# Table writes of an expert-routing kernel go through a queue: one per turn, in steps 3 and 7 of a batch

## The chip, the cores and the metric

One core of a Trainium2 chip runs the whole program. The metric is the device time of one execution in microseconds; lower is better.

## What is computed

The input is `x` (32 batches of 112 tokens of width 256) and a context of 375 rows per batch. A gated cross-attention with 16 heads of 64 is followed by a mixture of 8 experts with the two best experts per token:

```python
x = x + tanh(g_xattn) * xattn(ctx_1024, layernorm(x))     # keys, values: context and tokens, 487 rows
xf = layernorm(x).reshape(T, D)
gate_scores = softmax(xf @ gate_w)
topk_scores, topk_idx = top_k(gate_scores, 2)
topk_scores = topk_scores / sum(topk_scores)
h = gelu(xf @ w1[e] + b1[e]);  y = h @ w2[e] + b2[e]      # for the two experts of a token
out = x + tanh(g_ffn) * (topk_scores[0] * y[topk_idx[0]] + topk_scores[1] * y[topk_idx[1]])
```

## The kernel before

The program has two stages. The **attention stage** is one loop over `STEPS`; step t holds head pair t, that is pair t % 8 of batch t // 8 (`span(t)` gives batch b and pair j, both counted from 0). All engines run the same loop, each with its own part of the work of a step, in the order in which the code is written, and they meet at semaphores. In step t:

- TensorE makes the scores of pairs t and t+1 (t even, L1125), the K and V projections of the next batch (L1107) into two alternating banks `proj_ps`, and the product with V of pair t - 4 (L1156).
- ScalarE makes the exponentials (L639), a half-precision copy of them, `p_parts` high (L648), and copies K and V out of the projection banks (L694, L708).
- VectorE takes the minimum of the negated scores for the softmax (L864) and the low halves of K and V (L933, L939), which is what frees a projection bank.
- GpSimd makes the low half of the probabilities (`p_low_of`, L510), two pairs per even step; the exponential of pair p waits for the low half of pair p - 2. It also scales and splits the attention output (L530, L516) and does parts of the normalisation: the powers L552 (step 3 of a batch) and L579 (step 7).

Some 13 to 33 steps behind a batch's first step follow its output projection, second normalisation and routing: logits, the two best experts (`top`), and then, for a **group** of batches at once, the choice (`choose`, stage `hot`), a count of how many tokens chose each expert before this one (prefix matmuls, L1210 and L1212, stage `prefix`), and the row of each token in its expert's list (`rank_entries`, L888 to L900, stage `rank`). `GROUPS` (L83) says which batches form a group, `step_of` (L86) in which step a stage of a batch stands. The prefix matmuls of a group of n batches have widths 8(n+1), 8n, ..., 8.

The stage `entry` writes the routing table to DRAM: GpSimd issues, for each batch and each of the two choices k, one indirect DMA of 112 entries (L587), 64 in all. `entries_at` (L100) puts both writes of one batch of the group into each step from the group's entry step on. The addresses `place_i` and the values `entry` are kept for every batch separately until the end, and nothing reads the table before the last write has landed.

Steps 247 to about 276 run the last batches and at the same time load and split the expert weights (VectorE L906, ScalarE L667). Then the table is read (L593), and the **tile stage** runs the experts on tiles of 256 rows: gather (L599), two layers (L1256, L1280), and accumulating indirect writes (L615).

Of the kernel before, what the change touches and what calls it, by code (L numbers as in the profile page):

```python
# [13 lines left out]
NB, LQ, LC, D = 32, 112, 375, 256  # L14
# [5 lines left out]
NP = H // 2  # L20
KT = 4
INNER = H * DH
E, TOPK, F = 8, 2, 1024
# [24 lines left out]
STEPS = range(-3 * NP, NB * NP + 20)  # L48
PAIRS = NB * NP
# [30 lines left out]
EARLY = dict(zip(STAGES, (13, 14, 15, 16, 17, 18, 19, 20, 21, 22, 23, 23, 24, 25)))  # L80
LATE = dict(USUAL, hot=27, share=28, prefix=28, rank=29, entry=30)

GROUPS = ((0, 8), (8, 16), (16, 24), (24, 28), (28, 30), (30, 31), (31, 32))  # L83


def step_of(stage, b):  # L86

    return NP * b + (EARLY if b >= NB - 2 else LATE if b == NB - 3 else USUAL)[stage]
# [6 lines left out]
def groups_at(stage, t):  # L95

    return [n for n, (first, last) in enumerate(GROUPS) if step_of(stage, last - 1) == t]


def entries_at(t):  # L100

    return [first + t - step_of("entry", last - 1) for first, last in GROUPS if 0 <= t - step_of("entry", last - 1) < last - first]


PART_STEPS = sorted([NP * b + 5 for b in range(28)] + [NP * b + 1 for b in (4, 8, 12, 16)])
CHAIN = NP * 28

# [13 lines left out]
def program(nc, x, ctx_in, g_x, g_f, ln_m_g, ln_m_b, ln_l_g, ln_l_b, wq, wkv, wout, gate_w, w1, b1, w2, b2, out):  # L121
# [3 lines left out]
    table = dram("table_dram", [TABLE_ROWS, ROWS])  # L125
    with ExitStack() as st:  # L126
# [118 lines left out]
        place_i = sb("place_i", [128, NB, TOPK], I32)  # L245
        entry = sb("entry", [128, NB, TOPK, 2])
# [128 lines left out]
        def _(sp):  # L375
            def load(b):
                s = b % 2
                sp.dma_start(ctx_sb[0:CP, s], ctx_in[b].rearrange("(t p) d -> p t d", p=CP)).then_inc(ctx_loaded[s], 16)
                sp.dma_start(x_sb[0:LQ, s], x[b]).then_inc(ctx_loaded[s], 16)
# [33 lines left out]
            for t in STEPS:  # L413
# [17 lines left out]
                if j == 7 and b + 5 >= 2 and is_batch(b + 5):  # L431

                    sp.wait_ge(pool_step, subtracted(b + 3))
                    load(b + 5)
                if t + 2 in PART_STEPS:
                    n = PART_STEPS.index(t + 2)
                    if n >= 1:
# [38 lines left out]
        def _(pool):  # L476
# [42 lines left out]
            for t in STEPS:  # L519
# [14 lines left out]
                if j in (4, 6) and is_batch(nb):  # L534
                    k = (j - 4) // 2
# [9 lines left out]
                if j == 3 and is_batch(nb):  # L545
                    first = POOL_BASE + POOL_COUNT * nb
# [26 lines left out]
                for ob in batches_at("rstd2", t):  # L573
# [3 lines left out]
                    pool.tensor_tensor(rstd2[0:LQ, s, 0:1], moments2[0:LQ, s, 1:2], eps[0:LQ, 0:1], ALU.add).then_inc(rstd2_done, 1)  # L577
                    pool.wait_ge(rstd2_done, 2 * ob + 1)
                    pool.tensor_tensor(rstd2[0:LQ, s, 1:2], rstd2[0:LQ, s, 0:1], half[0:LQ, 0:1], ALU.pow).then_inc(rstd2_done, 1)  # L579
                for ob in entries_at(t):  # L580

                    n = [first <= ob < last for first, last in GROUPS].index(True)
                    if ob == 0:
                        pool.wait_ge(filled, 32)
                    pool.wait_ge(rank_done, n + 1)
                    for k in range(TOPK):
                        pool.indirect_dma_start(table.rearrange("r (n w) -> (r n) w", w=2), bass.IndirectOffsetOnAxis(ap=place_i[0:LQ, ob, k:k + 1], axis=0),  # L587
                                                entry[0:LQ, ob, k], None).then_inc(entered, 16)

            pool.wait_ge(row_known, 1)  # L590
            pool.wait_ge(entered, NB * TOPK * 16)
# [34 lines left out]
        def _(act):  # L626
# [42 lines left out]
            for t in STEPS:  # L669
# [51 lines left out]
                for n in groups_at("share", t):  # L721
                    first, last = GROUPS[n]
                    act.wait_ge(hot_done, n + 1)
# [36 lines left out]
        def _(dve):  # L760
# [106 lines left out]
            def choose(group):  # L867

                first, last = GROUPS[group]
                n = last - first  # L870
                if group >= 1:
# [3 lines left out]
                                         ALU.is_equal))  # L875
                if group >= 1 and n < GROUPS[group - 1][1] - GROUPS[group - 1][0]:
                    dve.memset(member[0:LQ, n], 0.0)
# [30 lines left out]
            for t in STEPS:  # L908
# [77 lines left out]
                if j == 1 and is_batch(nb):  # L986
# [7 lines left out]
                    last.then_inc(moments_done, 1)  # L994
                if t in PART_STEPS:
                    part = PART_STEPS.index(t)
                    dve.wait_ge(part_loaded, 32 * (part + 1))
# [313 lines left out]
```

## Time and profile before

| | |
|---|---|
| median of 3 runs | 1851.1 us (1851.03 to 1853.73) |
| profiled execution | 1851.1 us |
| its span | 1849.4 us |
| mean granted TensorE clock | 0.967 |
| attention stage, to the start of the tile stage | about 1440 us |
| tile stage | about 400 us |
| table writes (L587) | 64, from 514.1 to 1418.1 us |

The span runs from the first to the last instruction. A window's columns give each engine's busy time in it; a row of the timeline gives the start, the duration, the engine, the line, the operation with what it writes and reads, how many it merges, and in brackets the idle time of that engine before it and what ended it.

### The profile page before, as it was taken

To read this page: it belongs to the slowest core of one execution; us is meant where nothing else is said; L and a number is where in the kernel's file an instruction comes from. 1 tells how busy PE (TensorE), PEld (TensorE's weight loads), DVE (VectorE), ACT (ScalarE), POOL (GpSimd) and SP (SyncE) were. 2 spreads that over 40 slices of the span, in tenths; PEclk is the share of its full clock that TensorE was granted. 3 is DMA by queue.
4 is the path that set the end of the run, shared out by engine and by line. 5 is a ranking of instruction groups with operands and counts; after the bars stand their busy time and mean duration, and the time that the engine had idled before them with its cause. 6 is when DMAs were issued, how large, how long until landed. Compare 5 with 4: busy or idle time off the path is not lost. (4 is left out here: it accounts for less than half of the span.)

```text
span 1849.4 us, 42314 instructions
## 1 busy us (share of the span) xinstructions
PE 1670.0 (90%) x15044; PEld 1168.0 (63%) x15044; DVE 1307.3 (71%) x3059; ACT 1200.6 (65%) x2732; POOL 1259.7 (68%) x1350
## 2 busy tenths in 40 slices
PE   1899999999989999998999999999851899999995
PEld 0456666666655666665566666556541799999994
DVE  4677787777766877776677778677665676666662
ACT  2587777777767787776787777677753444444442
POOL 5377777877788877778877777886673355445542
PEclk9999999999999999999999999999965899999998
DMA  4177767677657677676676767555788133323334
GB/s 146 36 140 137 148 143 146 139 148 144 140 113 139 137 150 149 139 142 111 136 145 137 143 142 141 108 113 106 161 203 244 47 50 53 50 47 50 52 51 103
DMA packets 597544, 223.37 MB, mean 121 GB/s; under 512 B 535202, under 2 KB 587984, under 8 KB 596892
## 3 DMA queue, kind: packets, MB, share of 16 engines
q1 hardware_dynamic: 581804, 202.18, 52.1%
q0 software_dynamic: 15536, 18.49, 6.4%
q8 instruction: 126, 2.06, 0.5%
q14 instruction: 78, 0.64, 0.1%
HBM read 71.39 MB, written 20.76 MB: 50 GB/s over the span
## 5 line engine op out<-in xcount | busy, mean ns | idle before, releaser
L510 POOL TENSOR_TENSOR p_parts<-p_space,p_parts 112x487 f16<-112x487 f32 x512 | 559.8, 1117 | 167.3 <-ACT p_parts L648 166.8
L639 ACT ACTIVATE p_space<-scores_ps,shift 112x487 f32<-112x487 f32 x512 | 338.6, 665 | 46.4 <-POOL p_parts L510 44.5
L864 DVE TENSOR_SCALAR_CACHE_REDUCE passed<-scores_ps 112x487 f16<-112x487 f32 x512 | 308.6, 660 | 26.3 <-PE scores_ps L1125 25.9
L694 ACT ACTIVATE k_hi<-proj_ps 128x488 fp32r<-128x488 f32 x256 | 148.0, 578 | 256.3 <-PE proj_ps L1107 256.1
L939 DVE SCALAR_TENSOR_TENSOR v_sb<-proj_ps,v_sb 128x512 f16<-128x512 f32 (+1 forms) x256 | 176.9, 691 | 164.5 <-ACT v_sb L708 163.6
L648 ACT ACTIVATE p_parts<-p_space 112x487 f16<-112x487 f32 x512 | 276.3, 608 | 0.0
L744 ACT ACTIVATE o_space<-scores_ps,b_sb,undo 128x256 f32<-128x256 f32 x280 | 139.3, 560 | 206.3 <-PE scores_ps L1256 206.1
L615 POOL DMA_INDIRECT sums_dram<-pt_space,ot_space x70 | 117.5, 1679 | 183.7 <-ACT pt_space L754 170.2
L933 DVE TENSOR_TENSOR k_lo<-proj_ps,k_hi 128x488 fp32r<-128x488 f32 x256 | 169.6, 662 | 102.1 <-ACT k_hi L694 101.3
L1107 PE MATMUL proj_ps<-kv_hi,wkv_hi 128*128 128x488 f16 x512 | 192.3, 376 | 38.5 <-DVE v_sb L939 20.6
L1156 PE MATMUL pv_ps<-v_sb,pt_space 128*128 128x128 f16 x2048 | 218.1, 221 | 7.0 <-DVE o_space L985 6.0
L1107 PE MATMUL proj_ps<-wkv_hi,kv_hi 128*128 128x512 f16 (+1 forms) x512 | 196.5, 384 | 9.3 <-DVE v_sb L939 9.1
L1107 PE MATMUL proj_ps<-wkv_lo,kv_hi 128*128 128x512 f16 (+1 forms) x512 | 196.1, 383 | 0.0
L1107 PE MATMUL proj_ps<-wkv_hi,kv_lo 128*128 128x512 f16 (+1 forms) x512 | 196.0, 383 | 0.0
L1256 PE MATMUL scores_ps<-o_parts_space,arena 128*128 128x256 f16 x1680 | 191.9, 275 | 4.0 <-issue 2.2
L1107 PE MATMUL proj_ps<-kv_hi,wkv_lo 128*128 128x488 f16 x512 | 190.9, 373 | 0.0
L1107 PE MATMUL proj_ps<-kv_lo,wkv_hi 128*128 128x488 f16 x512 | 190.8, 373 | 0.0
L1280 PE MATMUL proj_ps<-arena,g_parts 128*128 x1680 | 189.0, 273 | 0.0
L1256 PEld LDWEIGHTS scores_ps<-o_parts_space,arena 128*128 x1680 | 165.6, 99 | 25.0 <-issue 4.7
L1280 PEld LDWEIGHTS proj_ps<-arena,g_parts 128*128 128x128 f16 x1680 | 164.4, 98 | 18.6
L708 ACT ACTIVATE v_sb<-proj_ps 128x512 f16<-128x512 f32 (+1 forms) x256 | 152.8, 597 | 15.7 <-PE proj_ps L1107 8.0
L1156 PEld LDWEIGHTS pv_ps<-v_sb,pt_space 128*128 128x128 f16 x2048 | 134.8, 99 | 36.9 <-issue 8.7
(218 smaller groups left out, 3552.5 us busy)
## 6 DMA issues: line engine op xcount, KB each, us to landing
w_part<-in_L_ffn_w_dram SPq DMA_DIRECT2D x64, 256.0 KB, 3.8
arena<-in_L_ffn_w_dram SPq DMA_DIRECT2D x28, 512.0 KB, 4.9
ctx_sb<-in_ctx_dram SPq DMA_DIRECT2D x32, 375.0 KB
pt_space<-p_parts SPq DMA_TRANSPOSE x256, 4.0
x_sb<-in_x_dram SPq DMA_DIRECT2D x32, 112.0 KB
res_sb<-in_x_dram SPq DMA_DIRECT2D x32, 112.0 KB, 5.2
sums_dram<-x_sb SPq DMA_DIRECT2D x32, 112.0 KB, 2.8
xn_dram<-xn_sb SPq DMA_DIRECT2D x32, 112.0 KB, 2.0
```

The source lines that it names most:

```text
L510: pool.tensor_tensor(p_parts[0:LQ, p % PS, h, 1, 0:LK], p_f[0:LQ, p % 2, h, 0:LK], p_parts[0:LQ, p % PS, h, 0, 0:LK], ALU.subtract).then_i ...
L639: act.activation(p_f[0:LQ, p % 2, h, 0:LK], scores_ps[n][0:LQ, 0:LK], ACT.Exp, bias=shift[0:LQ, p // 2 % 2, n:n + 1], scale=-1.0, accum_ou ...
L648: act.activation(p_parts[0:LQ, p % PS, h, 0, 0:LK], p_f[0:LQ, p % 2, h, 0:LK], ACT.Copy).then_inc(p_high, 1)
L694: act.activation(k_hi[:, j], ps[:, 0:LKP], ACT.Copy).then_inc(kq_high, 1)
L708: act.activation(v_sb[(b + 1) % 2][0:rows, c, 8 * half_:8 * half_ + 8, 0], ps[0:rows, :].rearrange("p (n d) -> p n d", d=DH), ACT.Copy, sc ...
L864: dve.tensor_scalar(passed[0:LQ, n, 0:LK], scores_ps[n][0:LQ, 0:LK], P_SHIFT, None, ALU.add, ALU.min, accum_out=shift[0:LQ, p // 2 % 2, n: ...
L933: dve.tensor_tensor(k_lo[:, j], ps[:, 0:LKP], k_hi[:, j].bitcast(F32), ALU.subtract).then_inc(kq_low, 1)
L939: dve.scalar_tensor_tensor(out=v_of(1), in0=ps[0:rows, :].rearrange("p (n d) -> p n d", d=DH), scalar=V_SCALE, in1=v_of(0), op0=ALU.mult, ...
L1107: last = nc.tensor.matmul(out, lhs(a, k), rhs(c, k), start=(n == 0), stop=(n == 3 * KD - 1))
L1156: last = nc.tensor.matmul(pv_ps[:, at:at + 128], block_of(0, c), v[:, c, n].rearrange("p a d -> p (a d)"), start=(c == 0), stop=(c == KT - 1))
L1256: last = nc.tensor.matmul(h_ps[m][:, c * ROWS:c * ROWS + ROWS], experts[:, bass.ds(e1, 1), at:at + 128].rearrange("p o f -> p (o f)"), (xt ...
L1280: last = nc.tensor.matmul(y_ps[s][:, r * D:r * D + D], g_parts[:, s, a, m, c * ROWS + r * 128:c * ROWS + r * 128 + 128], experts[:, bass.d ...
```

## The change

`entries_at` is replaced by a table `ENTRY_TURNS`. When a group's entry step comes, its writes, two per batch, are put at the end of a queue. In steps 3 and 7 of a batch one write leaves the queue (from step 208 on two), and from step 248 on up to four leave it in every step. Where a write is issued in a step, it stands at the same place of GpSimd's code as before. The groups are changed too: 16 to 24 and 24 to 28 become 16 to 22, 22 to 25 and 25 to 28.

```diff
-GROUPS = ((0, 8), (8, 16), (16, 24), (24, 28), (28, 30), (30, 31), (31, 32))
+GROUPS = ((0, 8), (8, 16), (16, 22), (22, 25), (25, 28), (28, 30), (30, 31), (31, 32))
...
-def entries_at(t):
-
-    return [first + t - step_of("entry", last - 1) for first, last in GROUPS if 0 <= t - step_of("entry", last - 1) < last - first]
-
-
+def entry_turns():
+
+    turns, waiting, ready = {}, [], {step_of("entry", last - 1): range(first, last) for first, last in GROUPS}
+    for t in STEPS:
+        waiting += [(ob, k) for ob in ready.get(t, ()) for k in range(TOPK)]
+        room = (1 if t < 208 else 2) if t % NP in (3, 7) else 0
+        if t >= PAIRS - NP:
+            room = 4
+        turns[t], waiting = waiting[:room], waiting[room:]
+    return turns
+
+
+ENTRY_TURNS = entry_turns()
...
-                for ob in entries_at(t):
+                for ob, k in ENTRY_TURNS[t]:
 
                     n = [first <= ob < last for first, last in GROUPS].index(True)
                     if ob == 0:
                         pool.wait_ge(filled, 32)
                     pool.wait_ge(rank_done, n + 1)
-                    for k in range(TOPK):
-                        pool.indirect_dma_start(table.rearrange("r (n w) -> (r n) w", w=2), bass.IndirectOffsetOnAxis(ap=place_i[0:LQ, ob, k:k + 1], axis=0),
-                                                entry[0:LQ, ob, k], None).then_inc(entered, 16)
+                    pool.indirect_dma_start(table.rearrange("r (n w) -> (r n) w", w=2), bass.IndirectOffsetOnAxis(ap=place_i[0:LQ, ob, k:k + 1], axis=0),
+                                            entry[0:LQ, ob, k], None).then_inc(entered, 16)
```

The writes of batches 0 to 7 stood in steps 89 to 96, those of 8 to 15 in 153 to 160, those of 16 to 23 in 217 to 224 and those of 24 to 27 in 249 to 252. Now there is one in each of the 30 turns of steps 91 to 207, two in each of the 10 turns of steps 211 to 247, four in step 249 and two in step 250. Those of batches 28 to 31 stay where they were, in steps 262 to 273 (batch 29 with 28 in step 262).

GpSimd, from step 89 on, before. A `DMA` row is a table write:

```order
L543 TENSOR_TENSOR norm_sb<-norm_sb,rstd 112x256
L587 DMA table_dram<-entry,place_i 32256x2 x2
L510 TENSOR_TENSOR p_parts<-p_space,p_parts 112x487 x2
L530 TENSOR_TENSOR o_space<-o_space,inv_sum 112x256
L510 TENSOR_TENSOR p_parts<-p_space,p_parts 112x487 x2
L516 TENSOR_TENSOR o_parts_space<-o_space,o_parts_space 112x256
L587 DMA table_dram<-entry,place_i 32256x2 x2
L548 TENSOR_SCALAR rstd<-moments 125x3
L550 TENSOR_SCALAR rstd<-moments 125x1
L552 TENSOR_TENSOR rstd<-rstd,half 125x4
L587 DMA table_dram<-entry,place_i 32256x2 x2
```

The same place in the changed kernel, whose line numbers from `p_low_of` on are 7 or 8 higher:

```order
L551 TENSOR_TENSOR norm_sb<-norm_sb,rstd 112x256
L518 TENSOR_TENSOR p_parts<-p_space,p_parts 112x487 x2
L538 TENSOR_TENSOR o_space<-o_space,inv_sum 112x256
L518 TENSOR_TENSOR p_parts<-p_space,p_parts 112x487 x2
L524 TENSOR_TENSOR o_parts_space<-o_space,o_parts_space 112x256
L556 TENSOR_SCALAR rstd<-moments 125x3
L558 TENSOR_SCALAR rstd<-moments 125x1
L560 TENSOR_TENSOR rstd<-rstd,half 125x4
L594 DMA table_dram<-entry,place_i 32256x2
```

Six writes stood between two powers of the normalisation; now one stands behind the second.

GpSimd in steps 249 to 252, before:

```order
L516 TENSOR_TENSOR o_parts_space<-o_space,o_parts_space 112x256
L587 DMA table_dram<-entry,place_i 32256x2 x2
L510 TENSOR_TENSOR p_parts<-p_space,p_parts 112x487 x2
L530 TENSOR_TENSOR o_space<-o_space,inv_sum 112x256
L510 TENSOR_TENSOR p_parts<-p_space,p_parts 112x487 x2
L516 TENSOR_TENSOR o_parts_space<-o_space,o_parts_space 112x256
L587 DMA table_dram<-entry,place_i 32256x2 x4
L510 TENSOR_TENSOR p_parts<-p_space,p_parts 112x487 x2
L530 TENSOR_TENSOR o_space<-o_space,inv_sum 112x256
L510 TENSOR_TENSOR p_parts<-p_space,p_parts 112x487 x2
L516 TENSOR_TENSOR o_parts_space<-o_space,o_parts_space 112x256
L587 DMA table_dram<-entry,place_i 32256x2 x2
```

and in the changed kernel:

```order
L524 TENSOR_TENSOR o_parts_space<-o_space,o_parts_space 112x256
L594 DMA table_dram<-entry,place_i 32256x2 x4
L518 TENSOR_TENSOR p_parts<-p_space,p_parts 112x487 x2
L538 TENSOR_TENSOR o_space<-o_space,inv_sum 112x256
L518 TENSOR_TENSOR p_parts<-p_space,p_parts 112x487 x2
L524 TENSOR_TENSOR o_parts_space<-o_space,o_parts_space 112x256
L594 DMA table_dram<-entry,place_i 32256x2 x2
L518 TENSOR_TENSOR p_parts<-p_space,p_parts 112x487 x2
L538 TENSOR_TENSOR o_space<-o_space,inv_sum 112x256
L518 TENSOR_TENSOR p_parts<-p_space,p_parts 112x487 x2
L524 TENSOR_TENSOR o_parts_space<-o_space,o_parts_space 112x256
```

Eight writes in three places became six in two.

## Rows read from the trace of the kernel before

**Rows 1.** The page: busy time of each engine, share of the span, instructions

```profile
PE 1670.0 (90%) x15044; PEld 1168.0 (63%) x15044; DVE 1307.3 (71%) x3059; ACT 1200.6 (65%) x2732; POOL 1259.7 (68%) x1350
```

**Rows 2.** Windows, one per batch: 14, 11, 12, 19, 20, 27, 28, 29, 16

```profile
core 0: us, PE busy (x) PEld busy (x) DVE busy (x) ACT busy (x) POOL busy (x), PEclk, DMA share, GB/s
634.80:674.00 39.20, 38.89 (x361) 25.05 (x358) 30.32 (x79) 30.80 (x73) 30.67 (x36) 1.00 0.70 141
...
503.80:550.60 46.80, 41.23 (x360) 25.55 (x358) 31.44 (x87) 31.18 (x73) 38.84 (x43) 0.96 0.57 107
550.60:595.60 45.00, 41.00 (x360) 25.62 (x358) 31.49 (x80) 31.25 (x74) 36.21 (x43) 0.96 0.74 139
...
833.10:878.80 45.70, 41.01 (x361) 25.53 (x360) 31.38 (x87) 31.18 (x73) 38.37 (x43) 0.96 0.62 111
878.80:922.40 43.60, 39.20 (x361) 25.00 (x360) 30.27 (x79) 31.06 (x74) 36.50 (x43) 1.00 0.65 136
...
1159.30:1205.00 45.70, 41.20 (x360) 25.68 (x358) 31.44 (x87) 31.17 (x73) 38.37 (x43) 0.96 0.60 108
1205.00:1249.30 44.30, 41.52 (x366) 26.46 (x364) 31.90 (x86) 31.11 (x74) 37.20 (x44) 0.96 0.56 107
1249.30:1289.80 40.50, 38.90 (x359) 25.06 (x358) 31.46 (x77) 30.80 (x73) 26.51 (x30) 1.00 0.58 111
...
713.20:753.00 39.80, 39.08 (x363) 25.14 (x360) 31.43 (x80) 30.80 (x73) 30.75 (x36) 1.00 0.76 155
```

**Rows 3.** Timeline at the head of the first burst: GpSimd, ScalarE, TensorE

```profile
514.11 1.21 POOL L587 DMA_INDIRECT table_dram<-entry,place_i  x1 [2.33 <-DVE entry L900]
515.62 0.95 POOL L587 DMA_INDIRECT table_dram<-entry,place_i  x1 [0.30 <-issue]
...
518.88 0.67 ACT L639 ACTIVATE p_space<-scores_ps,shift 112x487 f32<-112x487 f32 x1 [3.06 <-POOL p_parts L510]
...
520.90 0.54 PE L1107 MATMUL proj_ps<-kv_hi,wkv_hi 128*128 128x488 f16 x1 [1.97 <-DVE v_sb L939]
```

**Rows 4.** Timeline of undisturbed batches: GpSimd at steps 3 and 7, ScalarE after it

```profile
688.88 1.05 POOL L552 TENSOR_TENSOR rstd<-rstd,half 125x4 f32<-125x4 f32 x1
692.15 1.12 POOL L510 TENSOR_TENSOR p_parts<-p_space,p_parts 112x487 f16<-112x487 f32 x1 [2.23 <-ACT p_parts L648]
...
710.99 0.56 POOL L579 TENSOR_TENSOR rstd<-rstd,half 112x1 f32<-112x1 f32 x1
712.63 1.12 POOL L510 TENSOR_TENSOR p_parts<-p_space,p_parts 112x487 f16<-112x487 f32 x1 [1.09 <-ACT p_parts L648]
...
716.67 0.66 ACT L639 ACTIVATE p_space<-scores_ps,shift 112x487 f32<-112x487 f32 x1
```

**Rows 5.** Timeline of TensorE: prefix matmuls of batches 0 to 7, next scores

```profile
500.99 1.68 PE L1212 MATMUL tail_ps<-member,ones 112*112 112x64 f32 x16
...
503.82 0.48 PE L1125 MATMUL scores_ps<-k_hi,q_hi 64*112 64x488 f32 x2
```

**Rows 6.** Timeline of VectorE: first instruction of the rank chain, first behind it

```profile
511.23 0.21 DVE L888 COPY place<-tail_ps 112x64 f32<-112x64 f32 x1
...
513.08 0.66 DVE L933 TENSOR_TENSOR k_lo<-proj_ps,k_hi 128x488 fp32r<-128x488 f32 x1
```

**Rows 7.** Timeline of steps 249 to 252: GpSimd and ScalarE

```profile
1334.69 1.05 POOL L587 DMA_INDIRECT table_dram<-entry,place_i  x1 [2.02 <-DVE inv_sum L981]
...
1350.45 0.67 ACT L639 ACTIVATE p_space<-scores_ps,shift 112x487 f32<-112x487 f32 x1 [5.09 <-POOL p_parts L510]
...
1353.82 1.77 POOL L587 DMA_INDIRECT table_dram<-entry,place_i  x1 [0.16 <-issue]
```

**Rows 8.** One line's instructions (ns min/median/max), and the chain that ended last

```profile
L587 POOL DMA_INDIRECT table_dram<-entry,place_i x64: 938/947/3558, 514.1 to 1418.1; - x64
...
1418.07 1.74 POOL table_dram L587
1424.55 6.86 DMA ot_space<-table_dram,table_row
```

## The prediction

> **What bounds the kernel now.** The page comes first: TensorE is busy 90% of the span, the other engines 65 to 71% [rows 1]. An average over two stages says little of a change that sits in one, so the windows view is read next, one window per batch of 8 steps, each cut where the score matmuls of the batch's first head pair start (503.82 for one, [rows 5]). An undisturbed batch takes 39.2 us, of which TensorE is busy 38.89 at full clock, while VectorE, ScalarE and GpSimd are busy about 30 to 31 [rows 2]: there the attention stage runs at TensorE's pace. The batches in which a group of table writes is issued take 43.6 to 46.8 us, at a granted clock of 0.96 in most of them, and GpSimd's busy time in them rises to 36 to 39 us. TensorE is not what limits these.
>
> The timeline shows how. GpSimd reaches the first write of a group, waits 2.33 us for VectorE's rank chain, and then issues two writes, each 0.95 to 1.21 us with 0.30 us of issue between [rows 3]. Meanwhile the softmax split of the next head pair, which stands behind them on the same engine, is not done; ScalarE waits 3.06 us for it before its next exponential, the V copy behind that exponential is late, and TensorE waits 1.97 us for a free projection bank [rows 3]. The same is repeated in each of the following seven steps. Beside this stand the group's own costs, on other engines: TensorE's 18 small prefix matmuls (1.68 us for 16 of them, [rows 5]) and VectorE's rank chain, from 511.23 to 513.08, 1.85 us [rows 6].
>
> **The change, part by part.** All terms are against the profiled execution, 1851.1 us with a span of 1849.4; its time is also the median of the three runs.
>
> Bursts removed. The seven windows that hold the three bursts last 46.8 + 45.0 + 45.7 + 43.6 + 45.7 + 44.3 + 40.5 = 311.6 us; seven undisturbed ones would be 274.4 [rows 2]. The excess is 37.2 us. Not all of it is the writes'. One of these batches also holds an additional reduce of a weight part; the batch from 713.2, which has that reduce and nothing else, is 0.6 longer [rows 2]. The expert scales run beside the third burst: its last two windows are 0.7 and 1.3 longer than the window after the second burst and the undisturbed one, 2.0 in sum. That leaves 34.6 us for the writes and for the rank chain ahead of them. The rank chain is kept. Its price is between 0.6 (what a 1.2 us reduce costs in the batch from 713.2) and its full length plus the wait it ends, 1.85 + 2.33 = 4.2. I take 0.6, since in the changed kernel no write stands directly behind it: the first write of a group goes to step 3 of a batch, and the rank chain is in step 0. So the three bursts give back 34.6 - 3 x 0.6 = **32.8 us**.
>
> Single writes (30 turns, steps 91 to 207). At step 3 a write stands behind the power of the reciprocal deviation, and GpSimd is idle for 2.23 us there before the next split; at step 7 the idle time at the same place is 1.09 us [rows 4]. A write needs about 0.19 of issue and 0.95 to 1.05 of work [rows 3, 7]: it fits at step 3 and overruns at step 7 by some 0.1. Behind it, the exponential that needs this split starts at 716.67, and the split that begins at 712.63 and takes 2.2 us ends at 714.8 [rows 4]: 1.8 us of room. I charge nothing. If this cover were gone, 15 x 0.1 = 1.5 us.
>
> Double writes (10 turns, steps 211 to 247). A second write adds 0.30 + 0.94 [rows 3]: the overrun is 0.3 at step 3 and 1.35 at step 7. The 1.8 us of room takes it. Between 0 and 5 x 0.3 + 5 x 1.35 = 8.3 I take **+1**, near the lower end because of that room.
>
> Prefix and rank, TensorE and VectorE. Five large groups stand where four stood. The prefix matmuls go by total width: 360 columns for a group of eight (72 + 64 + ... + 8), about 1.75 us. The groups 16 to 24 and 24 to 28 had 360 + 120 columns, the new three have 224 + 80 + 80, so 96 fewer: -0.5 us. One additional rank chain on VectorE: +0.6, as above. Together **+0.1**. The queue never runs past its data: a group's results are kept for every batch, so a write that comes 60 steps late reads the same numbers.
>
> The end of the attention stage. Steps 249 to 252 had eight writes, now steps 249 and 250 have six (four, then two). Here GpSimd is the slow engine: ScalarE waits 5.09 us for it at 1350.45, after four writes in a row, and the writes beside the weight splits take up to 1.77 [rows 7]. The four writes at step 249 make the next pair 2.5 us later, the two fewer behind them give that back, and the pair after it has none where two took 1.77 + 0.30 + 0.94. That is up to 3.0 earlier at the last split. Behind it stands a chain of latencies (output projection, ranking of batch 31, the last two writes at 1418.07, the read of the table, [rows 8]) in which engines also wait for the expert weights. Between 0 and -3.0 I take **-1**.
>
> Sum: -32.8 + 0 + 1 + 0.1 - 1 = -32.7, so 1851.1 - 32.7 = **1818.4 us**. The second stage, the expert tiles, is untouched: its chain of scores and output matmuls only starts earlier.
>
> A rule to weigh against this: in the loop all writes took 0.94 to 1.21 us, while at 1353.82, beside VectorE's split of an expert weight, one took 1.77, and the longest of the 64 took 3.56 [rows 7, 8]. By that row the place of a write decides its price. The Trainium skill (SBUF — State Buffer, Who interferes with whom) says that GpSimd and VectorE share a port pair as an exclusive lock, so that a write's descriptors wait while certain VectorE instructions run; by that rule the spread writes, standing beside 40 different places of VectorE's work, could cost more than the bursts'. The trace agrees so far only for the expert splits, which begin at step 250.
>
> **The rivals.**
> (a) The overruns are not absorbed: each turn costs what it exceeds its gap by. 1.5 + 8.3 instead of 1 gives 1827.2. For: GpSimd and ScalarE wait for each other all through the loop. Against: the 1.8 us of room in [rows 4], and ScalarE's undisturbed exponentials have no wait for GpSimd. Chance 0.12.
> (b) The delay at the head of each burst is the rank chain's, not the writes': then 4.2 instead of 0.6 is kept for three groups and the new one, 4 x 3.6 = 14.4 more: 1832.8. For: the 2.33 us wait for VectorE. Against: GpSimd waits there only because a write is next. Chance 0.08.
> (c) Everything goes well: rank chains hidden (-1.8 - 0.6), doubles free (-1), the end gives 3.0 (-2): 1813.0. Chance 0.16.
> (d) Slower: each spread write meets a VectorE instruction that holds it up, as the one of 3.56. The overrun is then 3.56 + 0.19 - 1.09 = 2.7 at step 7 and 1.5 at step 3, over 20 turns each 84 us, and 10 second writes add 12: 1914. It decides from an overrun of 0.8 us per turn (32.7 / 40). Against: the write at the same place of step 3 inside the bursts took 1.05. Chance 0.02.
> (e) No change: what is gained before the end is lost there again, because the tail waits for the expert weights' transfers. Against: these start at step 247 and so move along. Chance 0.02.
>
> **How the numbers follow.** My forecast has 0.60. Its own range is 1815 to 1823. To hold 8 in 10 the range takes in (c) and (a): **1811 to 1829**; (b), (d) and (e) are left out. A measurement can tell about 0.2%, 3.7 us, from no change. Faster: 0.60 + 0.12 + 0.08 + 0.16 = 0.96, same 0.02, slower 0.02.
>
> **What would show it.** Batches 11, 12, 19, 20 and 27 at 39.2 to 41.5 us instead of 43.6 to 46.8, granted clock 1.00 in them; a write of 0.95 to 1.05 us directly behind the power at step 3 and 7; no exponential of ScalarE that waits for GpSimd before step 249; TensorE's prefix costing 1.7 us in batches 10 and 18, about 1.1 in batch 24. It would be wrong if undisturbed batches grew above 39.4 (then (a)), if writes in the loop took over 1.5 us (then (d)), or if TensorE waited over 1 us after a rank chain (then (b)).

## The result and the profile after

| | before | changed |
|---|---|---|
| median | 1852.4 us (1851.0 to 1855.1, 4 runs) | 1833.5 us (1829.3 to 1835.8, 4 runs) |
| profiled execution, its span | 1851.1, 1849.4 us | 1833.5, 1831.8 us |
| ratio to before | | 0.989, 95% interval 0.987 to 0.991 |
| mean granted TensorE clock | 0.967 | 0.972 |

The changed kernel is faster, but by 17.6 us of span where 32.7 were forecast; 1833.5 lies above the range of 1811 to 1829. So about 15 us have to be found. The page first, which answers to [rows 1]:

```profile
PE 1661.6 (91%) x15046; PEld 1164.5 (64%) x15046; DVE 1320.2 (72%) x3073; ACT 1199.8 (66%) x2733; POOL 1263.0 (69%) x1350
```

VectorE is busy 12.9 us longer than before with 14 instructions more. The added rank chain explains about 2 of it; the rest must be instructions that take longer. The windows, one per batch, cut as in [rows 2], here batches 11, 12, 19, 20, 25, 27, 28, 29 of the changed kernel:

```profile
502.70:544.50 41.80, 39.04 (x359) 25.07 (x358) 33.09 (x87) 30.82 (x73) 31.02 (x36) 1.00 0.61 127
544.50:584.20 39.70, 38.98 (x360) 25.09 (x358) 31.33 (x80) 30.80 (x73) 32.74 (x38) 1.00 0.76 153
...
821.60:863.50 41.90, 39.14 (x363) 25.13 (x360) 33.13 (x87) 30.81 (x73) 31.13 (x37) 1.00 0.67 128
863.50:902.70 39.20, 38.89 (x361) 25.07 (x360) 30.34 (x79) 30.80 (x73) 32.78 (x38) 1.00 0.71 141
...
1060.80:1102.60 41.80, 39.04 (x360) 25.08 (x358) 33.09 (x87) 30.82 (x73) 31.43 (x37) 1.00 0.64 128
...
1141.80:1182.80 41.00, 40.14 (x370) 25.78 (x368) 32.47 (x84) 31.09 (x74) 35.35 (x40) 1.00 0.68 130
1182.80:1225.10 42.30, 39.90 (x363) 25.58 (x362) 33.66 (x94) 31.03 (x73) 34.46 (x40) 1.00 0.56 108
1225.10:1270.30 45.20, 41.93 (x361) 26.14 (x358) 35.49 (x77) 31.13 (x73) 30.43 (x35) 0.92 0.55 100
```

The bursts are gone: 41.8 + 39.7 us where 46.8 + 45.0 stood, and the clock of batch 11 is 1.00 instead of 0.96. Batch 20, with two single writes, is at 39.2 exactly. But every batch with a rank chain (11, 19, 25, 28) keeps over 2 us, and batch 29, which had 40.5 before, is at 45.2 with a clock of 0.92.

Single writes stand where they were expected, behind the powers of steps 3 and 7 (timeline of GpSimd, batch 14; compare [rows 4]), and the split behind them is not late enough to matter:

```profile
638.29 1.05 POOL L560 TENSOR_TENSOR rstd<-rstd,half 125x4 f32<-125x4 f32 x1
639.54 1.05 POOL L594 DMA_INDIRECT table_dram<-entry,place_i  x1 [0.20 <-issue]
641.55 2.19 POOL L518 TENSOR_TENSOR p_parts<-p_space,p_parts 112x487 f16<-112x487 f32 x2 [0.96 <-ACT p_parts L655]
...
661.14 1.01 POOL L594 DMA_INDIRECT table_dram<-entry,place_i  x1 [0.20 <-issue]
662.18 2.20 POOL L518 TENSOR_TENSOR p_parts<-p_space,p_parts 112x487 f16<-112x487 f32 x2
```

Now the first rank chain, on VectorE, GpSimd and TensorE (compare [rows 3, 6]):

```profile
511.23 0.16 DVE L904 TENSOR_SCALAR ratio<-ratio 112x8 f32<-112x8 f32 x1
511.43 0.20 DVE L905 RECIPROCAL ratio<-ratio 112x8 f32<-112x8 f32 x1
511.67 0.81 DVE L906 TENSOR_SCALAR entry<-ratio,tanh_g 112x8 f32<-112x8 f32 x1
512.38 1.15 DVE L907 SCALAR_TENSOR_TENSOR entry<-ratio,tanh_g 112x8 f32<-112x8 f32 x1
513.45 0.65 DVE L940 TENSOR_TENSOR k_lo<-proj_ps,k_hi 128x488 fp32r<-128x488 f32 x1
...
511.32 2.19 POOL L518 TENSOR_TENSOR p_parts<-p_space,p_parts 112x487 f16<-112x487 f32 x2 [0.69 <-ACT p_parts L655]
...
514.16 0.38 PE L1114 MATMUL proj_ps<-kv_hi,wkv_hi 128*128 128x488 f16 x1 [1.65 <-DVE k_lo L940]
```

In the kernel before, the same two entry instructions took 0.23 us each, and the chain 1.85 us. Here they take 0.81 and 1.15 and the chain 3.36 (510.09 to 513.45). GpSimd's row is the pair of splits, 1.12 us each: L906 ends at 512.48, when the first of them does (512.44), and L907 at 513.53, with the second (513.51). K's low half comes late, and TensorE waits 1.65 us for its bank. Before, GpSimd stood still at this place, since its next item was a write that waited for this very chain.

The other place is the expert scales at step 231:

```profile
1224.38 0.94 POOL L594 DMA_INDIRECT table_dram<-entry,place_i  x1 [0.30 <-issue]
1225.34 2.21 POOL L518 TENSOR_TENSOR p_parts<-p_space,p_parts 112x487 f16<-112x487 f32 x2
1227.49 0.62 POOL L538 TENSOR_TENSOR o_space<-o_space,inv_sum 112x256 f32<-112x256 f32 x1
1228.06 2.17 POOL L518 TENSOR_TENSOR p_parts<-p_space,p_parts 112x487 f16<-112x487 f32 x2
...
1225.08 5.17 DVE L847 SCALAR_TENSOR_TENSOR peak_e<-peak_e 128x1 f32<-128x1 f32 x1
...
1231.03 0.61 PE L1114 MATMUL proj_ps<-wkv_hi,kv_hi 128*128 128x512 f16 x1 [2.95 <-DVE q_lo L931]
...
1231.58 0.67 ACT L646 ACTIVATE p_space<-scores_ps,shift 112x487 f32<-112x487 f32 x1 [2.90 <-DVE passed L871]
```

An instruction of one column takes 5.17 us, to the end of GpSimd's fourth split (1230.23). It took 1.05 before, and one of the same shape at the start of the program, with GpSimd idle, takes 0.16. TensorE waits 2.95 us, and its matmuls behind the wait take 0.61 instead of 0.38: the granted clock has gone down.

To compare kernels place by place, I take the time from the first score matmul of an even step to that of the next even step and subtract the undisturbed one (8.2, 10.2, 11.6 and 9.2 us, 39.2 in sum). This excess is also called the time over the pace. The excess, in us:

| place | before | changed |
|---|---|---|
| rank chains, from steps 90, 154, 202, 226 | inside the bursts | 2.6, 2.6, 2.6, 2.3 |
| expert scales, from steps 230 to 234 | 0.6 + 0 + 1.4 | 0.6 + 6.0 + 0 |
| two writes, from steps 216, 224, 240 | | 1.0, 0.3, 1.0 |
| two writes at steps 3 of a batch, and all single writes | | 0 |
| prefix matmuls after batch 18 | 1.8 + 1.0 | 1.3 + 0.8 + 0.8 |

The end of the attention stage (compare [rows 7, 8]):

```profile
1323.92 0.67 ACT L646 ACTIVATE p_space<-scores_ps,shift 112x487 f32<-112x487 f32 x1 [5.42 <-POOL p_parts L518]
...
L594 POOL DMA_INDIRECT table_dram<-entry,place_i x64: 938/1012/3568, 520.8 to 1399.8; - x64
```

The four writes in a row at step 249 cost ScalarE a wait of 5.42 us. From the start of batch 31 to the last table write it is 90.0 us, 89.5 before.

### The profile page after: what moved, and what is told of

Read it like the earlier page. It is cut to its first block and busy times, and to the rows that moved or that the text cites. A ratio compares the mean times of both kernels' runs of the same rounds, so it can differ in the third digit from the quotient of the medians.

```text
span 1831.8 us, 42337 instructions
## 1 busy us (share of the span) xinstructions
PE 1661.6 (91%) x15046; PEld 1164.5 (64%) x15046; DVE 1320.2 (72%) x3073; ACT 1199.8 (66%) x2733; POOL 1263.0 (69%) x1350
```

## The experiments

**Theory P**: VectorE's small instructions are held up while GpSimd runs beside them, and the change took away the places where GpSimd stood still. **Rivals**: a rank chain costs TensorE this much at its normal length (L); the second write of a turn costs it, by its own length or by the wait that each write now carries. The numbers E1 to E12 are the order of running; unless said otherwise, an edit is made to the changed kernel. A late signal is a completion signal of TensorE that the trace has more than 0.75 us after the start of its matmul. Their number in the attention stage depends on how signals and matmuls are paired: 18 to 22 in the kernels that have them by the pairing used below, 15 to 18 if each signal goes with the last matmul of its kind that had started. By either, the same kernels have them.

**GpSimd stands still beside the rank chain** (E2).

```diff
+                for n in groups_at("entry", t):
+                    pool.wait_ge(rank_done, n + 1)
                 for ob, k in ENTRY_TURNS[t]:
```

> The changed kernel, but GpSimd waits for the rank chain of a group at the place where the first write stood before (step 89 and its like), so that it stands still while VectorE computes that chain, and writes nothing there. Theory P (VectorE's small instructions are held up while GpSimd runs beside them): the rank chain takes 1.85 us again instead of 3.36, its last entries instructions 0.23 us instead of 0.81 and 1.15; the interval of step 90 falls from 2.6 us over the undisturbed pace to about 1.1, and with four large groups the time falls by up to 6 us. Rival L (the chain costs TensorE what it costs because it stands ahead of the K and V low halves, at any length): the interval stays at 2.6 and the time at 1833.5. Rival S (the standing still costs more than it spares, since the next split comes later): the interval grows above 3 and the time rises by 1 to 6 us.

Measured: 1824.4 us (1822.4 to 1830.2), ratio 0.987 (0.984 to 0.989). The timeline at the first rank chain:

```profile
511.86 0.23 DVE L908 TENSOR_SCALAR entry<-ratio,tanh_g 112x8 f32<-112x8 f32 x1
512.00 0.23 DVE L909 SCALAR_TENSOR_TENSOR entry<-ratio,tanh_g 112x8 f32<-112x8 f32 x1
...
512.31 2.18 POOL L518 TENSOR_TENSOR p_parts<-p_space,p_parts 112x487 f16<-112x487 f32 x2 [1.48 <-DVE entry L909]
...
512.86 0.38 PE L1116 MATMUL proj_ps<-kv_hi,wkv_hi 128*128 128x488 f16 x1 [0.15 <-DVE k_lo L942]
```

GpSimd is idle for 1.48 us here (0.69 in the changed kernel), and TensorE waits 0.15 instead of 1.65. The excess of the four intervals falls from 2.6, 2.6, 2.6, 2.3 to 1.1, 1.1, 1.0, 1.6. P holds, L and the rival of a costly standstill fall. What is left, 1.1, is the chain at its normal length. These four intervals give 5.3 of the 10.1 us by which the profiled execution is shorter than the changed kernel's. The rest is not the standstill's own: this run has no late signals, its clock stayed at 1.00 in the interval of the expert scales (see the next run), and its end was shorter. The instruction of the expert scales took 5.17 us again.

**The same kernel once more** (E10).

> The kernel in which GpSimd stands still beside the rank chains (second run), once more, for a second profile. It has a wait on every second write, and had no late completion signal of TensorE. If there are none again, late signals belong to the built program and not only to the wait; if there are about 20, they come and go from execution to execution. Rank chain 1.85 us, expert scales 5.17 us, span 1820 to 1824 in either case.

Measured: one run, 1827.2 us, span 1825.4 (1821.6 in the first profile). The rank chains are the same; no late signal in either. The interval of the expert scales is 6.0 us over the pace instead of 4.1, though the instruction takes 5.16. The windows of that interval in the first and in this profile:

```profile
1219.40:1231.70 12.30, 8.58 (x72) 4.75 (x70) 12.09 (x19) 7.13 (x17) 7.81 (x9) 1.00 0.46 94
```

```profile
1219.70:1233.90 14.20, 11.25 (x72) 5.91 (x70) 13.28 (x20) 7.16 (x17) 7.78 (x9) 0.76 0.40 81
```

The same 72 matmuls take 8.58 us at full clock and 11.25 at 0.76. So the same wait of TensorE was followed by 4.1 us over the pace in this interval at a clock of 1.00, and by 6.0 at 0.76. Part of that comes back at once: the next interval is 0.8 over the pace in the first profile and not at all in the second, so that the two cost 4.9 and 5.9 us together, and the lower clock about 1. This differs from execution to execution: in the changed kernel's profile the clock of this interval was 0.76 too, in its repetition (E6) 0.87.

**No write at step 231** (E5): two per turn from step 203, none at 231.

```diff
-        room = (1 if t < 208 else 2) if t % NP in (3, 7) else 0
+        room = (1 if t < 200 else 2) if t % NP in (3, 7) and t != 231 else 0
```

> The changed kernel, but no write leaves the queue in step 231, beside which VectorE computes the expert scales; the two writes are made up for by taking two per turn already from step 203. Theory P (a small VectorE instruction is held up as long as GpSimd runs without a gap): the 5.17 us of the one-column instruction of the expert scales goes back to about 1.05, the interval from step 232 falls from 6.0 us over the undisturbed pace to under 1.5, and the time falls by 4 to 5 us, to about 1829. Rival B (the two writes cost their own 2.4 us there and no more): the instruction still takes over 4 us and the gain is about 2.4 us. Two more turns of two writes at steps 203 and 207 cost 0 and about 1.

Measured: 1827.6 us (1825.2 to 1828.0), 4 to 6 below the changed kernel. Timeline and window:

```profile
1225.88 1.05 DVE L847 SCALAR_TENSOR_TENSOR peak_e<-peak_e 128x1 f32<-128x1 f32 x1
...
1224.73 2.19 POOL L518 TENSOR_TENSOR p_parts<-p_space,p_parts 112x487 f16<-112x487 f32 x2 [1.07 <-ACT p_parts L655]
```

```profile
1226.00:1266.50 40.50, 38.90 (x359) 25.05 (x358) 31.45 (x77) 30.79 (x73) 29.04 (x33) 1.00 0.61 112
```

The instruction takes 1.05 us, to the end of the split beside it (1226.92), and the batch is at the 40.5 us that it had before [rows 2]. Theory P again; rival B, 2.4 us, is too small: the intervals of the expert scales fall by 4.6 in sum. Two writes at steps 207, 215 and 239 cost 1.0 to 1.1 each, and at 203 nothing.

**One write at step 231** (E12).

```diff
-        room = (1 if t < 208 else 2) if t % NP in (3, 7) else 0
+        room = (1 if t < 207 or t == 231 else 2) if t % NP in (3, 7) else 0
```

> The changed kernel with one write in step 231 instead of two (one more is taken in step 207). In all traces with two writes there, the one-column instruction of the expert scales is asked for while GpSimd is at the second write, and takes 5.15 to 5.17 us, to the end of the fourth split behind it; without writes it is asked for during a split and takes 1.05 us, to the end of that split. Theory G (any back-to-back work of GpSimd holds it): with one write GpSimd still runs without a gap, and the instruction takes over 4 us again. Rival M (it matters that the request comes during a write): the request now falls into the split behind the single write, the instruction ends with that split or the next, in under 2.3 us, and step 232 loses its 4 to 6 us.

Measured: 1831.8 us in one run. On VectorE and GpSimd:

```profile
1228.41 3.92 DVE L847 SCALAR_TENSOR_TENSOR peak_e<-peak_e 128x1 f32<-128x1 f32 x1
...
1227.44 2.19 POOL L518 TENSOR_TENSOR p_parts<-p_space,p_parts 112x487 f16<-112x487 f32 x2
...
1230.15 2.16 POOL L518 TENSOR_TENSOR p_parts<-p_space,p_parts 112x487 f16<-112x487 f32 x2
```

It was asked for during the first split and still held to the end of the fourth (1232.31), 3.92 us; 4 was the bound of theory G, so it just misses the number, but the mechanism is G's, and M falls. The step was 2.8 us over the pace, at full clock. In this run both entry instructions of the fourth rank chain were held as well (1.01 and 1.14 us), and its interval was 4.1 over the pace, at a clock of 0.88; with both held and the clock at 1.00 (E1) it was 3.3, with one held (changed) 2.3, and with neither (E5, and the changed kernel's own repetition, E6) 1.3. The price of the same chain thus goes by where GpSimd's splits happen to stand, and differs between two executions of one program.

**The parts of the change by themselves.** The queue with the old groups (E3), and the old bursts with the new groups (E4):

```diff
-GROUPS = ((0, 8), (8, 16), (16, 22), (22, 25), (25, 28), (28, 30), (30, 31), (31, 32))
+GROUPS = ((0, 8), (8, 16), (16, 24), (24, 28), (28, 30), (30, 31), (31, 32))
```

> The changed kernel with the groups of the kernel before (8, 8, 8, 4), the queue alone. It has one rank chain and one prefix less than the changed kernel: if each of them costs TensorE what the trace shows (2.6 us for a chain, 0.8 to 1.3 for a small prefix), it is 1 to 3 us faster there; but the third group of eight comes due at step 217, so that the queue is longer at the end: the writes left at step 248 are then more than six, and the burst that is left at the end costs about 1.8 us per pair of them. Theory: between 1833 and 1840. Rival (groups do not matter): 1833.5 within 1 us.

Measured: 1831.5 us (1830.3 to 1834.8), ratio 0.990 (0.988 to 0.992), the changed kernel's. It saves a chain (2.6) and a prefix, and gives part of this back at the end: 3.2 us more than before between steps 248 and 254, with the four writes of step 249 and four in the next step. The median lies below both the 1833 to 1840 that were expected and the rival's 1832.5 to 1834.5. It is within 0.3 us of the changed kernel's repetition (E6, 1831.2), so the rival's statement stands though its number does not: no worth of the groups can be told here.

> The kernel before with the new groups alone, bursts as before. By the prediction's terms: prefix -0.5 and a rank chain +0.6, no change against 1852.4. By the trace of the changed kernel a rank chain and its prefixes cost more: +2.6 for the chain and about +0.9 for the smaller prefixes, and the burst of the middle is split up in three shorter ones: 1853 to 1856. If the groups save time (shorter bursts), it is under 1851.

Measured: 1850.6 us against 1851.5, ratio 1.000 (0.999 to 1.002). No change that can be told, as the prediction's terms had it; the 1853 to 1856 that the changed kernel's trace suggested did not come. Its profile shows six writes instead of eight in steps 249 to 252, and 86.2 us from the start of batch 31 to the last write against 89.5 before. All of the gain is the queue's.

**One wait per turn** (E1) instead of one per write.

```diff
+                if ENTRY_TURNS[t]:
...
+                    pool.wait_ge(rank_done, max([first <= ob < last for first, last in GROUPS].index(True) for ob, k in ENTRY_TURNS[t]) + 1)
                 for ob, k in ENTRY_TURNS[t]:
...
-                    pool.wait_ge(rank_done, n + 1)
```

> The changed kernel, but each turn of the queue waits once for the rank chain, ahead of its first write, where in the changed kernel every write has its own wait. In the trace of the changed kernel 18 completion signals of TensorE come more than 0.75 us late, all of them beside the second write of a turn, and none in the kernel before, where the second write of a pair has no wait of its own. Theory W (the wait on the second write delays them): no late signal is left, steps 216 and 240 lose their 1.0 us each, and the time falls by 2 to 4 us, to about 1830.5. Rival D (two writes in a row do it by themselves): the number of late signals stays near 18 and the time stays within 1 us of 1833.5.

Measured: 1830.7 us (1830.2 to 1831.8), ratio 0.989 (0.987 to 0.991). One late signal is left, and the excess of steps 216 and 240 goes from 1.0 and 1.0 to 0.6 and 0: theory W for the signals. The time decides nothing, since the changed kernel's repetition (E6) came to 1831.2. What a late signal looks like: ScalarE's copy of Q behind the last Q matmul at step 215, in the changed kernel and then here:

```profile
1143.23 0.63 ACT L689 ACTIVATE q_hi<-proj_ps,undo 128x448 fp32r<-128x448 f32 x1 [1.59 <-PE proj_ps L1114]
```

```profile
1142.50 0.64 ACT L689 ACTIVATE q_hi<-proj_ps,undo 128x448 fp32r<-128x448 f32 x1 [0.29 <-PE proj_ps L1114]
```

In the changed kernel the matmul started at 1141.67 and its signal is recorded 1.53 us later; elsewhere it comes after 0.23.

**The changed kernel once more** (E6).

> The changed kernel itself, once more. If the late completion signals of TensorE (18 of them above 0.75 us, none in four other kernels, two of which have the same waits on the second write) belong to the kernel, about 18 are there again, and steps 216 and 240 are each 1.0 us over the undisturbed pace; if they belong to that one execution, fewer than 3 are left, and the two steps are at 0.6 and 0. The rank chain (3.36 us) and the 5.17 us at step 231 stay in either case. Time 1830 to 1834.

Measured: 1831.2 us (1828.7 to 1833.8). 22 late signals, the steps at 1.1 and 1.1: they belong to the program, not to the execution. Three rank chains are at 2.6 again and the instruction of the expert scales takes 5.16 us; the fourth chain is at 1.3, with neither of its entry instructions held, and the interval from step 232 at 4.8, at a clock of 0.87. But over all 14 profiles (before, changed and twelve runs) the wait alone does not decide. With a wait on each write they are there in five (18 to 22: the changed kernel, E5, E6, E7, E8) and absent in four (E2, E3, E10, E12); without it there is one or none in all five (before, E1, E4, E9, E11). What else it takes is open. Here it is worth about 1.5 us. The same five profiles also have 17 to 20 signals that come 0.9 to 1.0 us after their matmul in the tile stage, whose code no run changes, and the other nine have none; so it is not the wait at the table writes that makes those late. They do not show in the time of the tile stage, 409.0 to 410.9 us with them and 409.2 to 411.0 without.

**All together** (E7): the standstill of E2, nothing at step 231, and two writes in steps 3 of a batch rather than 7.

```diff
-        room = (1 if t < 208 else 2) if t % NP in (3, 7) else 0
+        room = {3: 1 if t < 152 else 2, 7: {207: 2, 231: 0}.get(t, 1)}.get(t % NP, 0)
```

> The changed kernel with GpSimd standing still beside each rank chain, no write in step 231, and the queue's turns set so that two writes leave it in steps 3 of a batch (from step 155 on) and one in steps 7 (two at 207 alone). Theory P: rank chains at 1.1 us over the pace instead of 2.6 (four large groups, 2.3 to 1.6 at the fourth), step 232 under 1.5 instead of 6.0, no excess at steps 216 and 240: about 12 us below the changed kernel, 1820 to 1822. Rival (the parts do not add up, because what one spares another waits for): 1824 or more.

Measured: 1822.6 us (1821.5 to 1825.1), ratio 0.985 (0.982 to 0.987). Rank chains at 1.1, 1.1, 1.0, 1.6; the expert scales at 0.6 + 0 + 1.4; no excess but at the one step 7 that had two writes (1.0). The parts add up, though the median is 0.6 above the upper end of what was expected.

**At most two writes per step at the end** (E8): E7 with `room = 2` instead of 4 from step 248 on.

> As the run before, but at most two writes per step from step 248 on: the six at steps 249 and 250 become two each in steps 249, 250 and 251, and the four of step 262 two and two. In the changed kernel the six cost as much as the eight of the kernel before (steps 248 to 254 are 3.0 us under the undisturbed pace against 4.0 before). Theory T (four in a row make the split and the exponential behind them late, with no room to give it back): 1 to 2 us faster than the run before. Rival E (the end is set by the expert weights and their splits): within 0.5 us of it.

Measured: 1822.3 us (1820.6 to 1822.9). No difference: rival E. From the start of batch 31 to the last write it is 88.4 us, 87.8 in E7.

**And one wait per turn** (E9): E8 with the edit of E1.

> The kernel of the run before (GpSimd standing still beside the rank chains, nothing at step 231, two writes only in steps 3, at most two per step at the end), and in it one wait for the rank chain per turn instead of one per write. Theory W: with no wait on the second write there are no late completion signals of TensorE (18 to 20 above 0.75 us in the two runs before), the excess of 1.0 us at step 208 is gone or at 0.6, and the time is 0.5 to 1 us lower, 1821 to 1822. Rival: the late signals do not depend on the wait (two kernels with such waits had none): they stay.

Measured: 1821.6 us (1819.2 to 1824.4, 5 runs), ratio 0.984 (0.982 to 0.985). No late signal, step 208 at 0.6; the time is E8's within what can be told. Batches 11 and 29 in its windows:

```profile
502.20:542.50 40.30, 39.04 (x360) 25.05 (x360) 31.62 (x87) 30.93 (x73) 30.96 (x36) 1.00 0.64 132
1218.70:1259.30 40.60, 38.99 (x360) 25.09 (x358) 31.56 (x77) 30.80 (x73) 29.40 (x33) 1.00 0.61 111
```

This is the best version found: 1.6% below the kernel before and, by the medians, 12 us below the changed one (9.5 below its repetition).

**E9 with the old groups** (E11), ten writes instead of six in steps 248 to 252.

> As the ninth run, but with the groups of the kernel before (8, 8, 8, 4): one rank chain (1.1 us over the pace) and one small prefix fewer, two writes in steps 207 to 247 of kind 7, and ten writes instead of six in steps 248 to 252, two in each. By the prices measured so far: -1.1 for the chain, -1.3 -0.8 +1.8 for the prefixes, -1.6 +1.1 for the fourth chain, 0 to +1 for the ten writes: 0 to 2 us below the ninth run. Rival (the end of the attention stage pays for each write it is given): 1 to 3 us above it.

Measured: 1826.3 us (1824.7 to 1828.1), ratio 0.986 (0.984 to 0.987): 5 above E9, the rival's side and more. Up to batch 31 it is 1.4 us shorter, as the prices said (1223.4 against 1224.8 from the first scores). From there to the last write it takes 93.0 us against 87.6. So with everything else in order the smaller groups are worth something. That this is for the fewer writes at the end fits E4, where six instead of eight went with 3.3 us less; but only 1.3 of the 5.4 us are lost by TensorE's step 254, and how the writes would cost the rest behind that is not shown.

## Why the prediction was wrong

**Bursts removed, -32.8: right but for what they covered.** The seven windows fell to about the undisturbed pace, and single writes cost nothing at either place, 30 of 30. The step that failed is "I take 0.6, since in the changed kernel no write stands directly behind it". The kept rank chain costs 2.6, 2.6, 2.6 and 2.3 us instead of 4 times 0.6: **7.7 us** of the miss, of which 1 is chance, since the fourth came to 1.3 in the repetition (E6). Its normal length beside a still GpSimd would be 1.1 (E2); the other 1.5 is that the standstill, which I counted as loss only, had kept GpSimd from holding VectorE up. I had taken the price from a reduce beside a batch without delays, and the length 1.85 from a trace in which GpSimd waited: the row to read was its own wait, 2.33 us for this chain [rows 3]. The trace of the kernel before also shows the holding itself, in the choice of the first group and, with GpSimd idle, in that of the fourth:

```profile
488.18 1.32 DVE L878 TENSOR_TENSOR ratio<-max_v 112x8 f32<-112x8 f32 x1
...
487.88 1.59 POOL L559 TENSOR_TENSOR norm_sb<-ctx_sb,moments 125x768 f32<-125x768 f32 x1 [0.26 <-DVE kv_f L950]
...
1313.95 0.15 DVE L878 TENSOR_TENSOR ratio<-max_v 112x4 f32<-112x4 f32 x1
```

Beside GpSimd's subtraction the small instruction takes 1.32 us and ends with it, at 489.50 and 489.47; the other takes 0.15. The 1.05 us of the expert scales was a second such row.

**The expert scales, missing from the sum.** The second step that failed: I subtracted their 2.0 us as something that stays ("That leaves 34.6 us"). With two writes put ahead of them they cost 6.6: **4.6 us**, about 1 of it by the clock of this execution. I had listed the step for double writes with 1.8 us of room, measured at ScalarE, and had not looked at what VectorE does beside it.

**Double writes, +1.** The five at steps 3 cost nothing; of those at steps 7, one is the expert scales', one (step 247) is counted with the end, and three cost 1.0, 0.3 and 1.0: **1.3 us** over the forecast. Without the late signals the first costs 0.6 and the last nothing (E1), so the room was nearly as large as I had read it.

**Prefix and rank, +0.1.** The prefixes cost +0.1 instead of -0.5, **0.6 us**; the price does not go by columns alone.

**The end, -1.** To the last write +0.5, in a repetition (E6) -0.3: six writes with four in a row were no better than eight in pairs. From the last write to the end of the program this execution takes 0.7 longer, which is inside what the 14 profiles show there (431.3 to 434.2 us). So the end is **2.2 us** over the forecast. Before the first scores the changed kernel was 1.1 us earlier; over the 14 profiles that start lies between 73.0 and 75.9 us, so this is no effect of the change.

Sum: 7.7 + 4.6 + 1.3 + 0.6 + 2.2 - 1.1 = 15.3, and 15.1 are missing.

**The rivals.** (b) comes nearest in time, 1832.8, and its sign did appear: TensorE waits over 1 us after a rank chain. But its reason is not the measured one. It kept GpSimd's wait as the price, and in truth the missing of that wait is the price. (a) is refuted for 35 of 40 turns. (c) falls. (d) falls: writes in the loop take 0.94 to 1.05 us, the very first 1.22.

**The rule that I weighed.** I read the Trainium skill (SBUF — State Buffer, Who interferes with whom) only in the direction in which a GpSimd write is held by VectorE. The runs show the other one, in which GpSimd holds VectorE: L907 and L847, which read two tensors, were held beside the splits. This agrees with the Trainium skill's rule, in the same section, that a VectorE instruction with two SBUF inputs contends with a GpSimd one that reads SBUF. That only such instructions are held is not shown. L905, with a single input, took its 0.20 us beside the split, and L904 had started before it; but L906, with one tensor and a column, was held, and so was L789 with one tensor and a constant (0.57 us, to the end of GpSimd's L551, against 0.17 alone). The Trainium skill has the lock for one whole instruction; L906 and L907 fit that, L847 with its 5.17 and 3.92 us over four splits does not.

## What to carry to other kernels

A stall that a change removes may have been keeping two engines apart: before pricing what stays, list what the freed engine will now run beside it, and whether both use the same path to memory. Take the price of a small instruction from a row in which the neighbour is at work. When work is spread over many places, look up each place for a rare, short instruction of another engine that sits in a dependency chain; here one turn in forty cost a third of the miss, and leaving it out gave 4 to 6 us, while a deliberate standstill of GpSimd, 1.3 to 1.5 us at each of four places, made TensorE's interval 1.5 to 1.6 us shorter at three of them and 0.7 at the fourth, which in the changed kernel's repetition needed no standstill.

## What the runs showed of the hardware that was not expected

- A VectorE instruction of 112x8 elements (L906, L907) takes 0.23 us alone and 0.81 to 1.15 beside GpSimd's splits, ending with one of them. One of 128x1 (L847) took 5.15 to 5.17 us in six profiles and 3.92 in one, each time to the end of the fourth of four splits, but 1.04 or 1.05 in the seven profiles in which GpSimd had been idle for about 1.1 us just ahead of the splits. Why it gets its turn at the end of the second split in the one case and only behind the fourth in the other was not found.
- The same wait of 3 us on TensorE was followed by a granted clock of 1.00 or 0.76 over the same interval in two executions of one kernel (E2, E10). The lower clock made this interval 1.9 us longer and, with the next one, about 1 in all; no other difference was found there.
- Completion signals of TensorE came up to 2.7 us after the start of their matmul, beside the second and later table write of a turn, in five of the nine profiles of kernels that have a wait on each of these writes; of the five profiles without it none has more than one. The same five have late signals in the tile stage too, whose code is the same. Two executions of one program agree, both where signals are late (changed, E6) and where none is (E2, E10), so it hangs on the built program; the condition is open.
